# One program for attention, routing scores and experts, with one plan of memory and the first routed tiles turned in attention's tail

## The chip, the cores and the metric

The kernel runs on one core of a Trainium2 chip. The metric is the device time of one execution in microseconds; less is better. A core has five engines that run their own instruction queues and meet through semaphores: TensorE (PE; matmuls and transposes), VectorE (DVE), ScalarE (ACT), GpSimd (POOL) and SyncE (SP), which here issues nearly all transfers (DMAs) between DRAM and the core's memory, SBUF. Results of TensorE land in PSUM, eight banks of 128 partitions by 512 fp32 numbers.

## The reference

Input x is 4 batches of 1024 tokens of 512 numbers, fp32 throughout.

```python
# attention, 16 heads of 32, with biases; then residual and layernorm
x = _layernorm(x + _L0_attn_ref(x, wq, bq, wk, bk, wv, bv, wo, bo))
# routed and shared feed-forward
scores = xf @ gate_w.T                      # 8 experts
ew, ei = jax.lax.top_k(scores, 2); ew = softmax(ew)
expert_out = (silu(xf @ w_gate[e].T) * (xf @ w_up[e].T)) @ w_down[e].T   # H = 256
routed = weighted sum of the two chosen experts
shared = silu(xf @ sh_gate.T) * (xf @ sh_up.T) @ sh_down.T               # HS = 512
sgate = sigmoid(xf @ se_gate_w.T)
x = _layernorm(x + routed + sgate * shared)
```

## The kernel before

Tokens are handled in tiles of 128, TT = 32 tiles in all, eight (KT) to a batch. Where precision matters, an operand is split into a high part of a faster format and the low remainder, and three matmuls take the place of one.

The kernel is a row of programs, each a `nc.Block` of its own: inside a block the engines run freely by semaphores, and a block ends for all engines together before the next one begins. SBUF and PSUM of a stage are given back at its end and handed out anew to the next.

**Attention** (`attention`, L117 on). Per batch, four groups g of four heads (16 key steps of four slots each: `batch` on each engine), then a tail. SyncE's order is written out by hand in `body` and `tail`: projections' inputs, row sums out and their reciprocals back (`few`, `invert`, L384 to L396), the stacked keys and queries. In the last batch the output weights, kept in DRAM as high and low part (one megabyte each), are fetched at the end of group 1 into x_hi and x_lo (L433). In the tail, TensorE makes eight output tiles, 12 matmuls each (`o_tile`, L734 to L737). For every tile VectorE adds the residual and takes statistics (L1021 to L1029), GpSimd raises the variance to the power -0.5 and makes the shift (L561, L563), ScalarE normalises (L876), and SyncE stores it to x2 in DRAM (`store`, L460). The first four tiles of the last batch are kept in probs_mid. SyncE ends with a wait for all stores.

**Identity.** A small block of `moe` makes a second identity matrix on GpSimd (L2062, L2064).

**Routing scores** (`scores`). Tiles are taken four at a time, eight groups q. SyncE loads x2's tiles into four slots x_r (L1139). TensorE turns a tile by four transposes (`turn`, L1178, into pr_t). ScalarE copies the high part (`high`, L1227), VectorE subtracts for the low part (`low`, L1250). TensorE then makes the scores of four tiles with 12 matmuls (`score`, L1189), VectorE copies them (L1259), TensorE turns them back (`back`, L1200), and VectorE reads them into `route` (L1263). TensorE's order is written out in `group`: turn the next four tiles, scores of these, back of the last four. SyncE's order: router matrix (9 rows, L1142), tiles 0 to 3, one megabyte of shared weights (L1145), tiles 4 to 7, the other two megabytes (L1150), the rest of the tiles, each as its slot has been turned. GpSimd clears the router matrix (L1158) and splits the shared weights, 12 pieces of two operations (L1164, L1166). At the end ScalarE takes one tanh for the shared gate (L1241).

**Feed-forward** (`feed_forward`). SyncE loads tiles 0 to 3 into x_t (L1457), then eight experts' weights, twelve megabytes (L1474, L1475). Twelve tiles of the shared part (COVER = 12) run on TensorE: `turn` (L1572), `up` (24 matmuls, L1578), `down` (12), `turn_hidden` (L1603). Beside them VectorE chooses experts and builds the table of which token sits in which slot (`first_choice` and so on, from L1893), in many small operations. Then come 71 tiles of experts, in order of expert, and the other 20 shared tiles, with the results gathered and normalised.

## Time and profile before

| | us |
|---|---|
| median of 3 runs | 2098.14 (2097.38 to 2098.63) |
| the profiled execution's own time | 2099.2 |
| its span, first to last instruction | 2097.5 |
| TensorE busy | 2018.8 |
| VectorE busy | 1278.3 |
| ScalarE busy | 880.3 |
| GpSimd busy | 868.1 |

Mean granted clock of TensorE: 0.988 of full speed. Times in the trace count from the first instruction. The profile tells for each instruction its line, engine, start and duration, and for idle time in brackets how long the engine had been idle and what it waited for. In the rows, L12 is line 12 of the kernel; `out<-in` are the tensors written and read. A row with x4 merges four instructions in a row. A row of a stage gives its length, then the busy time of PE, PE's weight loads, DVE, ACT and POOL, and then three numbers: TensorE's granted clock (1.00 is 2.4 GHz, 0.50 is 1.2 GHz), the busy share of the 16 DMA engines, and what they moved in GB/s.

### The profile page before, as it was taken

To read this page: it belongs to the slowest core of one execution; us is meant where nothing else is said; L and a number is where in the kernel's file an instruction comes from. 1 tells how busy PE (TensorE), PEld (TensorE's weight loads), DVE (VectorE), ACT (ScalarE), POOL (GpSimd) and SP (SyncE) were. 2 spreads that over 40 slices of the span, in tenths; PEclk is the share of its full clock that TensorE was granted. 3 is DMA by queue.
4 is the path that set the end of the run, shared out by engine and by line. 5 is a ranking of instruction groups with operands and counts; after the bars stand their busy time and mean duration, and the time that the engine had idled before them with its cause. 6 is when DMAs were issued, how large, how long until landed. Compare 5 with 4: busy or idle time off the path is not lost. (4 is left out here: it accounts for less than half of the span.)

```text
span 2097.5 us, 30323 instructions
## 1 busy us (share of the span) xinstructions
PE 2018.8 (96%) x9764; PEld 1226.9 (58%) x9765; DVE 1278.3 (61%) x2281; ACT 880.3 (42%) x1563; POOL 868.1 (41%) x831
## 2 busy tenths in 40 slices
PE   7999999999999999999999986899999999999997
PEld 5655556655556655556655435588544444447886
DVE  5777775777776677775677855574222222225875
ACT  2266664466664466663466672321111111112332
POOL 3255654556654556653554555200111111114651
PEclk9999999999999999999999998999999999999999
DMA  7322434331434231335131305642222222225752
GB/s 231 71 53 55 100 78 107 115 69 42 101 76 131 92 76 47 97 67 163 60 77 33 91 12 201 221 186 66 90 90 88 86 87 89 90 80 166 229 175 74
DMA packets 95923, 213.00 MB, mean 102 GB/s; under 512 B 24305, under 2 KB 24817, under 8 KB 92593
## 3 DMA queue, kind: packets, MB, share of 16 engines
q1 hardware_dynamic: 84992, 175.96, 28.3%
q0 software_dynamic: 10800, 35.40, 6.2%
q8 instruction: 70, 1.15, 0.2%
q14 instruction: 61, 0.49, 0.1%
HBM read 118.51 MB, written 41.93 MB: 76 GB/s over the span
## 5 line engine op out<-in xcount | busy, mean ns | idle before, releaser
L947 DVE TENSOR_REDUCE max_half<-ps_side 128x1 f32<-128x512 f32 x1024 | 658.2, 682 | 204.6 <-PE ps_side L666 201.4
L666 PE MATMUL ps_side<-kq_stack 96*128 96x512 f32 x1024 | 409.4, 404 | 4.9 <-DVE max_half L947 2.4
L688 PE MATMUL ps_s<-kq_stack 97*128 97x512 f32 x937 | 393.0, 420 | 8.0 <-ACT probs_first L843 5.1
L688 PEld LDWEIGHTS ps_s<-kq_stack 97*128 97x128 f32 x937 | 177.8, 190 | 165.0 <-issue 85.5
L1636 PE MATMUL ps_gu<-gu_sb,xT_e 128*128 x568 | 257.7, 596 | 0.5 <-issue 0.3
L1534 POOL DMA_INDIRECT x_g<-x,who_all x71 | 67.3, 948 | 454.7 <-PE ps_t L1626 358.4
L843 ACT ACTIVATE probs_first<-ps_s 128x512 f32<-128x512 f32 x326 | 187.6, 600 | 106.0 <-PE ps_s L688 90.5
L666 PEld LDWEIGHTS ps_side<-kq_stack 96*128 96x128 f32 x1024 | 195.2, 191 | 57.8 <-DVE max_half L947 26.5
L843 ACT ACTIVATE probs_mid<-ps_s 128x512 f32<-128x512 f32 x308 | 177.5, 599 | 112.0 <-PE ps_s L688 97.4
L590 POOL TENSOR_TENSOR acc<-probs_first,probs_mid 128x512 f32<-128x512 f32 x129 | 163.8, 1297 | 133.2 <-ACT probs_mid L843 133.2
L843 ACT ACTIVATE probs_last<-ps_s 128x512 f32<-128x512 f32 x303 | 175.5, 599 | 97.2 <-PE ps_s L688 81.0
L590 POOL TENSOR_TENSOR acc<-probs_last,probs_first 128x512 f32<-128x512 f32 x129 | 163.3, 1292 | 116.6 <-ACT probs_first L843 116.6
L590 POOL TENSOR_TENSOR acc<-probs_mid,probs_last 128x512 f32<-128x512 f32 x118 | 149.6, 1295 | 109.8 <-ACT probs_last L843 109.4
L1757 ACT ACTIVATE act_g<-ps_gu 128x256 f32<-128x256 f32 x71 | 27.2, 383 | 346.6 <-PE ps_gu L1636 346.6
L1834 DVE TENSOR_TENSOR hid<-act_g,ps_gu 128x256 f32<-128x256 f32 x71 | 29.9, 421 | 221.7 <-ACT act_g L1757 221.7
L1636 PEld LDWEIGHTS ps_gu<-gu_sb,xT_e 128*128 128x128 f32 x568 | 102.3, 190 | 106.3 <-issue 106.0
L712 PE MATMUL ps_sum<-acc,ones 128*32 128x512 f32 x1024 | 134.7, 597 | 8.9 <-DVE acc L982 4.9
L1659 PE MATMUL ps_d<-wd_sb,act_g 128*128 x284 | 133.7, 593 | 0.5 <-DVE act_g L1841 0.5
L640 PE MATMUL ps_side<-x_hi,wkq_hi 128*128 128x512 f32 x256 | 103.0, 402 | 12.1 <-DVE x_lo L1036 10.5
L1847 DVE COPY y_t<-ps_d 128x512 f32<-128x512 f32 x71 | 49.1, 691 | 93.5 <-PE ps_d L1659 93.5
L1578 PE MATMUL ps_gu<-sgu_hi,xT_hi 128*128 128x512 f32 x256 | 104.0, 406 | 1.5 <-DVE xT_lo L1804 1.5
L640 PE MATMUL ps_side<-x_lo,wkq_hi 128*128 128x512 f32 x256 | 102.2, 399 | 0.0
(237 smaller groups left out, 3312.0 us busy)
## 6 DMA issues: line engine op xcount, KB each, us to landing
kq_stack<-kq SPq DMA_DIRECT2D x192, 256.0 KB, 5.1
y_slots<-y_t SPq DMA_DIRECT2D x71, 256.0 KB, 2.3
x_r<-x SPq DMA_DIRECT2D x32, 256.0 KB, 3.7
x_t<-x SPq DMA_DIRECT2D x32, 256.0 KB, 2.9
gu_sb<-wgu SPq DMA_DIRECT2D x8, 1024.0 KB, 16.1
out<-gu_sb SPq DMA_DIRECT2D x32, 256.0 KB, 2.7
res<-inv_rows SPq DMA_DIRECT2D x124, 64.0 KB, 2.0
stage<-wkqT SPq DMA_DIRECT2D x28, 256.0 KB, 3.0
```

Source lines behind the costliest of these rows:

```text
L590: nc.gpsimd.tensor_tensor(acc[:, h, :], probs(loc - 1, h), probs(loc, h), ALU.add).then_inc(folded, 1)
L640: done = nc.tensor.matmul(bank, w, xs, start=r == 0, stop=r == UNIT - 1)
L666: nc.tensor.matmul(bank, q_stack[par][0:3 * HD, h, t * P:(t + 1) * P], k_stack[par][0:3 * HD, h, half * HALF:(half + 1) * HALF], start=Tru ...
L688: nc.tensor.matmul(out, k_stack[par][0:3 * HD + 1, h, kt * P:(kt + 1) * P], q_stack[par][0:3 * HD + 1, h, half * HALF:(half + 1) * HALF], ...
L712: done = nc.tensor.matmul(ps_sum[h * HD:(h + 1) * HD, :], ones[:], acc[:, h, :], start=kt == FOLD - 1, stop=kt == KT - 1)
L843: nc.scalar.activation(probs(loc, h), score_bank(b, loc * HG + h)[0], ACT.Exp, scale=HD ** -0.5).then_inc(probs_ready, 1)
L947: nc.vector.reduce_max(max_half[:, u // 2, u % 2:u % 2 + 1], bank, AX.X).then_inc(side_free, 1)
L1534: nc.gpsimd.indirect_dma_start(x_g[:, t % 4, :], None, x2, bass.IndirectOffsetOnAxis(ap=who_all[:, t:t + 1].bitcast(U32), axis=0),).then_i ...
L1578: done = nc.tensor.matmul(out, w, m, start=c == 0 and i == 0, stop=c == last_c and i == 2)
L1636: done = nc.tensor.matmul(ps_gu[:, s % 2, :], e_xT[:, s % 2, c, :], gu_sb[:, bass.ds(e, 1), c, :].rearrange("p a n -> p (a n)"), start=c = ...
L1659: done = nc.tensor.matmul(ps_d[:, s % 2, :], e_hT[:, s % 2, c, :], wd_sb[:, bass.ds(e, 1), c, :].rearrange("p a n -> p (a n)"), start=c == ...
L1847: nc.vector.tensor_copy(y_t[:, s, :], ps_d[:, s % 2, :]).then_inc(ey_done, 1)
```

## The change

All stages stand in one block. Each engine's program is the three stages' programs one behind the other, with no meeting of engines between them. Memory is given out for routing and feed-forward first, and attention's buffers are laid over the same addresses in an order chosen so that what the next stages need early lies over what attention is done with early. One identity matrix serves all.

Of the work around the old joins, this is moved:

- In the last batch the output weights are fetched at the beginning of group 3 (`load_last`), into the keys' part of kq_stack0. Behind them, in the same place, come the router matrix and tiles 0 to 3 for the routing scores.
- In attention's last tail SyncE issues the first megabyte of shared weights ahead of the stores, the loads of tiles 4 to 7 behind the store of output tile 5, tiles 8 to 11 behind the last store, then the other two megabytes and the rest of the routed tiles.
- TensorE turns routed tiles 0 to 7 behind the eighth output tile. ScalarE copies their high parts: tiles 0 to 3 behind the normalisation of output tile 5, tiles 4 to 7 behind that of tile 7. VectorE makes the low parts behind its last output tile, and the router matrix's low part behind output tile 2.
- The eight groups of `scores` start with the scores of tiles 0 to 3 and turn tiles from group 1 on.
- The output tiles 0 to 3 of the last batch are kept in place in probs_first (`res_of`).
- Feed-forward's first four tiles are loaded as routed tiles 28 to 31 have been turned; its expert weights behind the last split of the shared weights.

```diff
-def attention(nc, x, xT, wkqT, wvT, woT, bq, bk, bv, bo, x2, passed):
+def attention(nc, keep, block, ident, router, x, xT, wkqT, wvT, woT, bq, bk, bv, bo, x2, passed):
...
-        def res_of(t):
-            return probs_mid[:, t, :] if t < 4 else x_of(t)
-        block = ctx.enter_context(nc.Block())
+        def res_of(b, t):
+            return probs_mid[:, t, :] if t < 4 and b < B - 1 else x_of(t)
...
+            def load_r(t):
+                sp.dma_start(router.x_t[:, t % 4, :], x2[t // KT, t % KT * P:(t % KT + 1) * P, :]).then_inc(
+                    router.x_in[t % 4], 16)
+
+            def load_shared(k):
+                sp.dma_start(router.stage[:, k], router.shared[k]).then_inc(router.st_in[k], 16)
+
+            def load_last(b):
+                sp.wait_ge(scores_ready, b * HEADS_B + (G - 1) * STEPS * HG)
+                sp.sem_inc(passed, 1)
+                for i, part in enumerate(wo_last):
+                    sp.dma_start(part.bitcast(F32), wo_kept[i]).then_inc(wo_in, 16)
+                sp.wait_ge(router.rw_zero, 1)
+                sp.dma_start(router.rw_raw[:, :, 0:E + 1], router.rw).then_inc(router.rw_in, 16)
+                for t in range(4):
+                    sp.wait_ge(x2_out[t], 16 * 2)
+                    load_r(t)
+
             def body(b, m, g, last):
+                if last and g == G - 1:
+                    load_last(b)
...
-                if last and g == 1:
-                    sp.wait_ge(proj_ready, PROJ * B * G)
-                    sp.sem_inc(passed_sp, 1)
-                    for i, part in enumerate((x_hi, x_lo)):
-                        sp.dma_start(part[:, :, 0:D].bitcast(F32), wo_kept[i]).then_inc(wo_in, 16)
...
                 load_x_nat(b, 3, res[:])
-                for t in range(KT):
+                if not last:
+                    for t in range(KT):
+                        store(b, t)
+                    return
+                sp.wait_ge(scores_ready, B * HEADS_B)
+                sp.sem_inc(passed, 1)
+                load_shared(0)
+                for t in range(6):
                     store(b, t)
+                for t in range(4, 8):
+                    sp.wait_ge(router.t_ready, t - 3)
+                    load_r(t)
+                for t in range(6, KT):
+                    store(b, t)
+                for t in range(8, 12):
+                    sp.wait_ge(router.t_ready, t - 3)
+                    load_r(t)
+                for k in range(1, 3):
+                    load_shared(k)
+                for t in range(12, TT):
+                    if t >= (B - 1) * KT:
+                        sp.wait_ge(x2_out[t % KT], 16 * (B + 1))
+                    sp.wait_ge(router.t_ready, t - 3)
+                    load_r(t)
...
-            for t in range(KT):
-                sp.wait_ge(x2_out[t], 16 * (B + 1))
...
+                    if last and g == G - 1 and at == 0:
+                        pool.wait_ge(proj_ready, PROJ * B * G)
+                        nc.gpsimd.memset(router.rw_raw[:], 0.0).then_inc(router.rw_zero, 1)
...
             for t in range(KT):
                 o_tile(b * TAIL + KT + t, b, t, tail_bank(t),
-                       [x_hi[:, g, 0:D] for g in range(G)], [x_lo[:, g, 0:D] for g in range(G)])
+                       [wo_last[0][:, g, :] for g in range(G)], [wo_last[1][:, g, :] for g in range(G)])
+            pe.wait_ge(probs_ready, B * HEADS_B)
+            pe.wait_ge(ctx_taken, INVERSES)
+            pe.wait_ge(sum_taken, INVERSES)
+            for q in range(2):
+                for s in range(4):
+                    router.turn(pe, q, s)
+            pe.wait_ge(tail_free, B * TAIL)
...
+            act.wait_ge(router.rw_in, 16)
+            nc.scalar.activation(router.rw_hi[:], router.rw_raw[:], ACT.Copy).then_inc(router.rw_high, 1)
             for t in range(KT):
                 norm(B - 1, t)
+                if t == 5:
+                    for s in range(4):
+                        router.high(act, 0, 0, s)
+            for s in range(4):
+                router.high(act, 1, 1, s)
...
                 if t < 2:
                     ctx_low_last(t)
+                if t == 2:
+                    dve.wait_ge(router.rw_high, 1)
+                    nc.vector.tensor_tensor(router.rw_lo[:], router.rw_raw[:], router.rw_hi[:].bitcast(F32),
+                                            ALU.subtract).then_inc(router.rw_split, 1)
+            for q in range(2):
+                for s in range(4):
+                    router.low(dve, q, q, s)
...
+class Router:
+    def turn(self, pe, q, s):
+        t = 4 * q + s
+        pe.wait_ge(self.x_in[s], 16 * (q + 1))
+        if not static(q, 1):
+            pe.wait_ge(self.t_hi, t - 3)
+            pe.wait_ge(self.t_lo, t - 3)
+        for c in range(C):
+            done = self.nc.tensor.transpose(self.ps_t[:, s, c * P:(c + 1) * P], self.x_t[:, s, c * P:(c + 1) * P],
+                                            self.ident[:])
+        done.then_inc(self.t_ready, 1)
...
-        block = ctx.enter_context(nc.Block())
...
             for t in range(4):
+                sp.wait_ge(router.t_ready, TT - 3 + t)
                 load_tile(t)
+            sp.wait_ge(router.st_split, 3 * C)
+            sp.sem_inc(passed, 1)
             for e in range(E):
...
+        with nc.Block() as block:
+            attention(nc, keep, block, ident, router, x, xT, wkqT, wvT, woT, bq, bk, bv, bo,
+                      x2.rearrange("(b s) d -> b s d", b=B), passed)
+            scores(nc, block, router, weights_hi_lo, route, sgate_all, ident, passed)
+            feed_forward(nc, keep, block, router, memory, x2, sgu_hi, sgu_lo, sd_hi, sd_lo, wgu, wd, base, y, gu_sb,
+                         wd_sb, route, sgate_all, weights, pos, tile_expert, ident, out, passed)
```

## Rows read from the trace of the kernel before

**Rows 1.** The page, part 1: busy us, share of the span, instructions.

```profile
PE 2018.8 (96%) x9764; PEld 1226.9 (58%) x9765; DVE 1278.3 (61%) x2281; ACT 880.3 (42%) x1563; POOL 868.1 (41%) x831
```

**Rows 2.** Busy time by stage, from:to, length, PE, PEld, DVE, ACT, POOL, clock, DMA, GB/s.

```profile
1283.60:1294.80 11.20, 0.01 (x1) 0.01 (x1) 2.01 (x6) 1.88 (x3) 1.52 (x6) 0.70 0.33 94
1294.80:1314.82 20.02, 15.89 (x76) 10.26 (x77) 8.93 (x14) 7.17 (x12) 13.51 (x16) 0.82 0.90 339
1314.82:1344.87 30.05, 29.37 (x182) 17.42 (x180) 17.64 (x34) 10.51 (x20) 8.59 (x9) 1.00 0.47 146
1344.87:1351.16 6.29, 1.12 (x5) 0.75 (x5) 1.22 (x4) 1.71 (x3) 2.38 (x6) 0.61 0.67 197
1351.16:1359.17 8.01, 8.01 (x24) 6.33 (x25) 2.80 (x8) 0.43 (x1) 0.00 (x0) 0.67 1.01 411
```

**Rows 3.** The chain that ended last: start us, us, work; a later feed-forward tile.

```profile
1404.66 5.54 PE ps_gu L1578 x24
```

**Rows 4.** TensorE in order of time at the first join: start us, us, work.

```profile
1282.50 1.07 PE L737 MATMUL ps_side<-x_lo,kq 128*128 128x512 f32 x4
...
1294.79 1.12 PE L1178 MATMUL pr_t<-ident_m,x_r 128*128 128x128 f32 x4 [11.22 <-DMA x_r<-x]
...
1296.07 2.66 PE L1178 MATMUL pr_t<-ident_m,x_r 128*128 128x128 f32 x12 [0.16 <-DMA x_r<-x]
...
1309.18 2.58 PE L1178 MATMUL pr_t<-ident_m,x_r 128*128 128x128 f32 x16 [1.33 <-DMA x_r<-x]
...
1311.52 0.48 PE L1189 MATMUL pr_s<-xT_hi_r,rw_hi 128*16 128x512 f32 x1
...
1314.82 2.28 PE L1178 MATMUL pr_t<-ident_m,x_r 128*128 128x128 f32 x16
```

**Rows 5.** VectorE and ScalarE in order of time, first join and a steady group.

```profile
1283.60 0.69 DVE L1021 TENSOR_TENSOR res<-ps_side,res 128x512 f32<-128x512 f32 x1 [0.76 <-PE ps_side L737]
...
1285.41 0.14 DVE L1029 TENSOR_SCALAR var_eps<-mv 128x1 f32<-128x1 f32 x1
...
1286.49 0.81 ACT L876 ACTIVATE res<-res,shift,rstd 128x512 f32<-128x512 f32 x1 [1.90 <-POOL shift L563]
...
1315.51 2.22 ACT L1227 ACTIVATE xT_hi_r<-pr_t 128x512 fp32r<-128x512 f32 x4 [3.12 <-PE pr_t L1178]
...
1316.14 2.48 DVE L1250 TENSOR_TENSOR xT_lo_r<-pr_t,xT_hi_r 128x512 fp32r<-128x512 f32 x4 [0.78 <-ACT xT_hi_r L1227]
```

**Rows 6.** The routed tiles' loads (x_r), from issue to landing.

```profile
DMA to landing us min/median/max: 2.6/3.7/6.9
```

**Rows 7.** Busy time in single microseconds, columns as in rows 2.

```profile
1288.00:1289.00 1.00, 0.00 (x0) 0.00 (x0) 0.00 (x0) 0.00 (x0) 0.00 (x0) 0.59 0.70 262
...
1298.00:1299.00 1.00, 0.72 (x5) 0.48 (x3) 0.84 (x2) 0.84 (x2) 0.00 (x0) 0.79 1.00 422
```

**Rows 8.** Busy time in a stretch full of transfers, columns as in rows 2.

```profile
1295.00:1308.00 13.00, 10.07 (x44) 6.94 (x43) 5.64 (x9) 4.78 (x8) 7.01 (x8) 0.74 1.02 399
```

**Rows 9.** GpSimd in order of time: the last splitting operation of the shared weights.

```profile
1322.43 1.30 POOL L1166 TENSOR_TENSOR sd_lo<-wd_sb,sd_hi 128x512 fp32r<-128x512 f32 x1
```

**Rows 10.** ScalarE and TensorE in order of time at the second join.

```profile
1345.13 0.26 ACT L1241 ACTIVATE th<-route 128x32 f32<-128x32 f32 x1 [6.95 <-DVE route L1263]
...
1348.54 1.12 PE L1572 MATMUL ps_t<-ident_m,x_t 128*128 128x128 f32 x4 [3.68 <-DMA x_t<-x]
...
1349.69 0.60 ACT L1730 ACTIVATE xT_hi<-ps_t 128x512 fp32r<-128x512 f32 x1 [4.30 <-PE ps_t L1572]
```

**Rows 11.** SyncE's queue and VectorE in the last group of attention.

```profile
1213.07 3.07 SPq L384 DMA_DIRECT2D sum_few<-res  x4
...
1227.02 0.24 DVE L970 RECIPROCAL inv_few<-sum_few 128x16 f32<-128x16 f32 x1
```

**Rows 12.** Groups by line (page, part 5): ScalarE's exponentials by target buffer.

```profile
L843 ACT ACTIVATE probs_first<-ps_s 128x512 f32<-128x512 f32 x326 | 187.6, 600 | 106.0 <-PE ps_s L688 90.5
...
L843 ACT ACTIVATE probs_mid<-ps_s 128x512 f32<-128x512 f32 x308 | 177.5, 599 | 112.0 <-PE ps_s L688 97.4
```

More of the change, by code:

```diff
@@ new lines, in attention @@
+        kq_stack = [sb(f"kq_stack{i}", [P, 2, HG, S], F32R) for i in range(2)]
+        x_hi = sb("x_hi", [P, C, S], F32R)
+        x_lo = sb("x_lo", [P, C, S], F32R)
+        wkq_hi = sb("wkq_hi", [P, 2, C, P], F32R)
+        wkq_lo = sb("wkq_lo", [P, 2, C, P], F32R)
+        wv_hi = sb("wv_hi", [P, C, D], F32R)
+        acc, wo_hi = twin("acc", "wo_hi", [P, HG, HALF])
+        v_sb = sb("v_sb", [P, KT, D])
+        probs_last, wo_lo = twin("probs_last", "wo_lo", [P, HG, HALF])
+        probs_mid, wv_lo = twin("probs_mid", "wv_lo", [P, HG, HALF])
@@ new lines, in sem @@
+            return keep.enter_context(nc.semaphore(name))
+        self.nc, self.ident, self.stage, self.shared, self.rw = nc, ident, stage, shared, rw
+        self.x_t = sb("x_r", [P, 4, D])
+        self.rw_raw = sb("rw_raw", [P, C, RW])
+        self.rw_hi = sb("rw_hi", [P, C, RW], F32R)
+        self.rw_lo = sb("rw_lo", [P, C, RW], F32R)
+        self.xT_hi = sb("xT_hi_r", [P, 2, C, 4 * P], F32R)
+        self.xT_lo = sb("xT_lo_r", [P, 2, C, 4 * P], F32R)
+        self.sT = sb("sT", [RW, 2, 4 * P])
@@ new lines, in __init__ @@
+        self.th = sb("th", [P, TT])
+        self.ps_t = space.enter_context(nc.psum_tensor("pr_t", [P, 4, D], F32))
+        self.ps_s = space.enter_context(nc.psum_tensor("pr_s", [P, 2, 4 * P], F32))
+        self.ps_b = space.enter_context(nc.psum_tensor("pr_b", [P, 4, RW], F32))
+        self.st_in = [sem(f"st_in{i}") for i in range(3)]
+        self.st_high = sem("st_high")
+        self.st_split = sem("st_split")
+        self.rw_zero, self.rw_in, self.rw_high, self.rw_split = [
+            sem(f"rw_{n}") for n in ("zero", "in", "high", "split")]
@@ L1169, in _ @@
         def _(pe):
-            def turn(q, s):
-                t = 4 * q + s
-                pe.wait_ge(x_in[s], 16 * (q + 1))
-                if not static(q, 1):
-                    pe.wait_ge(t_hi, t - 3)
-                    pe.wait_ge(t_lo, t - 3)
-                for c in range(C):
-                    done = nc.tensor.transpose(ps_t[:, s, c * P:(c + 1) * P], x_t[:, s, c * P:(c + 1) * P], ident[:])
-                done.then_inc(t_ready, 1)
             def score(q, g):
@@ L1203, in group @@
             def group(q, g, first, last):
+                if not first and not last:
+                    for s in range(4):
+                        r.turn(pe, q + 1, s)
                 if first:
-                    for s in range(4):
-                        turn(q, s)
-                if not last:
-                    for s in range(4):
-                        turn(q + 1, s)
-                if first:
-                    pe.wait_ge(rw_split, 1)
+                    pe.wait_ge(r.rw_split, 1)
                 score(q, g)
@@ L1265, in group @@
             def group(q, g, first, last):
-                if first:
-                    low(q, g)
-                if not last:
-                    low(q + 1, 1 - g)
+                if not first and not last:
+                    for s in range(4):
+                        r.low(dve, q + 1, 1 - g, s)
                 take(q, g)
@@ L1584, in up @@
                 pe.wait_ge(t_lo, t + 1)
+                if t == 0:
+                    pe.wait_ge(router.st_split, 2 * C)
                 if t >= 1:
```

320 lines of the change are left out of this document (136 added, 184 removed).

## The prediction

> **What bounds the kernel now.** First the page: TensorE is busy for 96% of the span [rows 1]. That is an average over stages, so the next view is the table of busy time by stage, cut at the two joins which the change touches [rows 2]. Its first row runs from the end of the last output matmul to the first transpose of the routing scores. It is 11.2 us long and TensorE has nothing in it. In the second row (20.0 us up to the fourth group of scores) TensorE works 15.9 us, at a mean clock of 0.82. The third row is steady: busy 29.4 of 30.05 us, full clock. The fourth and fifth are the second join, 6.3 us with 1.1 us of work and then 8.0 us of matmuls at a mean clock of 0.67, where a later tile takes 5.5 us for the same 24 [rows 3]. Away from the joins TensorE is the bound, and the change leaves its matmuls as they are. So the question is how much of these 45.5 us (11.2 + 20.0 + 6.3 + 8.0) remains.
>
> **First join, before.** The output matmuls end at 1283.57. Transposes of routed tile 0 begin at 1294.79, of tiles 8 to 11 at 1309.18; the second scores begin at 1311.52, and turning tiles 12 to 15 at 1314.82 [rows 4]. Ahead of it stand VectorE's statistics of the last output tile, ScalarE's normalisation at 1286.49, its store, the barrier, the identity, and only then the loads [rows 4, 5].
>
> **First join, after, on the clock of the old trace.**
> 1. *Tiles 0 to 3.* Their rows in DRAM are two batches old, and SyncE fetches them in the last group of attention. TensorE turns them right behind the last output matmul. Twelve transposes at half clock took 2.66 us, so sixteen at full clock take 1.8, and sixteen in a steady group, with waits in them, 2.28 [rows 4]. These wait for nothing, so I take 1.8: 1283.6 to 1285.4.
> 2. *Tiles 4 to 7* need their slot loaded again. SyncE issues a load when the transpose of its slot is done, 1284.2 for the first. x_r loads landed in 2.6 to 6.9 us, 3.7 at the median [rows 6]. The long ones stood behind a megabyte of weights, and that megabyte (shared weights, part 0) now moves behind the last input load of the tail, well before. I take 2.9 us, near the low end: 1287.1, then one each 0.5 us. The transposes also need the slot's low half off VectorE, which is free at 1285.55 [rows 5] and does four in 2.48 [rows 5]: 1286.2 to 1288.1. So 1287.1 to 1289.2. The bounds are 2.6 and 6.9 us: 0.3 us better, 4 us worse.
> 3. *ScalarE* puts four copies (2.22 us, [rows 5]) ahead of the normalisation of output tile 6. It waits for the first transposes at 1284.2, is done at 1286.4, and normalises tiles 6 and 7 by 1288.0, where tile 7 ended at 1287.3. Behind these two stand only their stores and the loads of tiles 8 to 11, issued from 1288.6 to 1290.1 and landed by 1293.2. TensorE wants them about then.
> 4. *First scores*, 12 matmuls. The second ones with the four small transposes back took 3.30 [rows 4], of which the transposes are some 0.35, so 2.95 alone. The clock: after 4.6 us without work it was at half from about 1288.2 [rows 7]. The new gap has transposes in it, 1.8 us and then 2 us of thinly spread ones in 5.6 us. I expect the clock to fall once and to be back within these scores: 3.8 us, 1289.2 to 1293.0. With a clock that holds it would be 2.95, with a low one to the end twice that, 5.9; I stay nearer to the first, since the work no longer stops.
> 5. *Tiles 8 to 11, scores 1, back:* 2.34 + 3.30 as before [rows 4], to 1298.6.
> 6. *Tiles 12 to 15* are issued behind the other two megabytes of shared weights (issued at 1290.6). At 399 GB/s [rows 8] these take 5.3 us, to about 1296.5, and tiles 12 to 15 are there from 1297.6 to 1299.6. That just fits, at a bound of 2 us if it does not. Turning of tiles 12 to 15 starts at 1298.6, not at 1314.82: **16.2 us gained**.
>
> From there the group is TensorE's own, as in the third row of [rows 2].
>
> GpSimd's 24 splitting operations of the shared weights ended at 1323.7 [rows 9]. They now begin at about 1286.5 instead of 1300.7 and pause for the second megabyte, so they end near 1313 and nobody waits. VectorE's one small subtraction (0.23 us) behind output tile 2 and ScalarE's 0.26 us copy lie in slack: VectorE idled 0.76 us ahead of the last tile [rows 5]. Cost nothing.
>
> **Second join.** Before: the scores end at 1344.87, the loads of the feed-forward tiles are issued only behind the barrier, tile 0 is turned at 1348.54, ScalarE copies at 1349.69, VectorE subtracts, and the first matmul starts at 1351.16, 1.47 us behind the copy's start [rows 2, 10]. Now the four loads are issued while tiles 28 to 31 are turned, more than one group of 5 us (the third of [rows 2] holds six) ahead of the end, and the last lands in time unless it takes the whole 6.9. TensorE turns tile 0 at once: four transposes, 0.5 us, to 1345.4. ScalarE has its tanh at 1345.13 for 0.26 [rows 10] and is free. It copies from 1345.4, and 1.47 us on the first matmul starts, at 1346.9: **4.3 us gained**. The 24 matmuls took 8.0 us at a mean clock of 0.67, and take 5.54 at full clock [rows 2, 3]: **2.4 us more** if the clock holds. TensorE stands for 1.5 us there, behind four transposes; before, it stood for 3.68 [rows 10], and the clock fell. I count some chance that it falls again for part of the matmuls, and take 1.9. VectorE's first choice of experts (with the subtraction 2.80 us and more in the last row of [rows 2]) still fits under 5.5 us of matmuls. The twelve megabytes of expert weights start some 10 us earlier by the same clock, behind the four tile loads and the splitting. They are needed twelve shared tiles later, so this earns nothing and delays nothing.
>
> **What moves inside attention.** SyncE's queue of the last batch gets seven transfers (two megabytes of output weights, one of routed tiles, the small router matrix) ahead of the row-sum transfers which it issued at 1213.07. Issue costs some 4 us. The three megabytes at 399 GB/s need 7.9 us [rows 8, 11]. So the sums arrive at about 1222, and VectorE takes their reciprocal at 1227.02, without having waited [rows 11]. About 5 us of cover remain; each microsecond over it would hold VectorE and with it TensorE. GpSimd's clearing of the router matrix is 0.15 us. Cost nothing.
>
> **Sum:** 16.2 + 4.3 + 1.9 = 22.4 us off the profiled execution, whose span is 2097.5 and whose time is 2099.2. The median of the runs is 1.06 lower than that execution, 2098.14; less 22.4 gives **2075.7 us**. By the bounds of steps 2, 4 and 6 and of the second join the gain lies between 16 and 25.
>
> The Trainium skill, TensorE: Matmul & The Clock Gate, "Part 4: PE-mode transpose", says that the engine's transposes do not count as activity for the clock. The trace speaks against it here: between 1294.8 and 1298.9 TensorE ran transposes alone, and the clock went from half to full at about 1298.4 [rows 4, 7]. By the page the first scores would run wholly at half clock (5.9 us for 3.8), and the gain would be 2.1 us smaller; by the row I leave it.
>
> **Rivals.**
> - *The loads replace the barrier* (chance 0.13). Tiles 4 to 7 land at the median or later, or tiles 12 to 15 wait for the weights, and both joins run at half clock. For: in the second row of [rows 2] the transfer engines are 0.90 busy. Against: the first megabyte has left that stretch. Price 5 us or so: gain 17.4, 2080.7.
> - *The row sums come late* (0.04). Three megabytes stand ahead of them; if they took twice the estimate, the sums would come at about 1230, plus the time to reach the next reader: 3 to 10 us lost, 2079 to 2086. Against: nothing else of size moves there.
> - *Placement* (0.03), the slower side. All attention buffers have other addresses. If the long stage, 1283.6 us, ran slower by 1.75% or more, the whole gain would be gone; at 2.2% the time would be 2103.9. Against: ScalarE's exponentials into different buffers take 600 and 599 ns [rows 12].
> - *The joins do not open* (0.02): some wait still orders the engines as the barrier did, by SyncE's order of stores and loads. Then the time stays within 4 us of 2098.
>
> **Numbers.** The forecast has 0.78, its own range 2072.5 to 2079. The range of 8 in 10 takes in most of the first rival: 2071.5 to 2081. A difference of 0.2%, some 4.2 us, is about what a measurement of this kernel can tell from none. Faster by more than that hold the forecast, the first rival and most of the second, 0.95; within it 0.02; slower 0.03.
>
> **What would show it.** Right: the time from the last output matmul to the turning of tile 12 falls from 31.25 to about 15 us, no wait of pr_t on x_r over 3 us; the scores' end to the end of the first 24 matmuls falls from 14.3 to about 8; attention ends where it did, at 1283.6, with the reciprocal at about 1227 not waiting. Wrong: DVE idle ahead of inv_few in the last group, a second long wait on x_r, a clock at half into the second group of scores, or exponentials off 600 ns.

## The result, and the profile after

The changed kernel takes **2083.45 us** by the median of four runs (2079.12 to 2085.13), beside 2098.39 for the kernel before on the same chip: a ratio of 0.9925 with a 95% interval of 0.9909 to 0.994, or 15 us less. Forecast were 2075.7, range 2071.5 to 2081.0. The profiled execution is the fastest of the four, 2079.12 us with a span of 2077.4, so it must not be set against the forecast by itself.

The page's part 1 of the changed kernel, which answers to [rows 1]:

```profile
PE 2010.8 (97%) x9764; PEld 1220.1 (59%) x9765; DVE 1278.2 (62%) x2281; ACT 880.1 (42%) x1563; POOL 868.2 (42%) x829
```

The same 9764 matmuls run. TensorE in order of time at the first join, as in [rows 4]; the value in brackets is the idle time ahead and what ended it:

```profile
1277.07 1.07 PE L771 MATMUL ps_side<-kq_stack,kq 128*128 128x512 f32 x4
1277.98 1.91 PE L1197 MATMUL pr_t<-ident,x_r 128*128 128x128 f32 x16
1281.16 1.35 PE L1197 MATMUL pr_t<-ident,x_r 128*128 128x128 f32 x8 [1.27 <-DMA x_r<-x]
1283.88 1.97 PE L1197 MATMUL pr_t<-ident,x_r 128*128 128x128 f32 x8 [1.37 <-DMA x_r<-x]
1285.50 0.78 PE L1249 MATMUL pr_s<-xT_hi_r,rw_hi 128*16 128x512 f32 x1
...
1289.14 1.91 PE L1197 MATMUL pr_t<-ident,x_r 128*128 128x128 f32 x16
...
1295.71 2.95 PE L1197 MATMUL pr_t<-ident,x_r 128*128 128x128 f32 x16 [1.53 <-DMA x_r<-x]
...
1302.79 1.97 PE L1197 MATMUL pr_t<-ident,x_r 128*128 128x128 f32 x16
```

The 11.2 us without work are gone: the first sixteen transposes stand right behind the last output matmul. In their place are three shorter waits, all put down to the rows of routed tiles (4 and 5, 6 and 7, 12 to 15). SyncE's queue in the same stretch, and the busy time by windows (columns as in [rows 2]):

```profile
1278.61 1.74 SPq L394 DMA_DIRECT2D x_r<-x  x4
1281.40 1.02 SPq L493 DMA_DIRECT2D x<-res  x2
1282.47 3.73 SPq L394 DMA_DIRECT2D x_r<-x  x4
1286.24 1.11 SPq L398 DMA_DIRECT2D wd_sb<-shu  x1
1287.40 0.43 SPq L398 DMA_DIRECT2D wd_sb<-shd  x1
1289.77 1.86 SPq L394 DMA_DIRECT2D x_r<-x  x4
```

```profile
1278.00:1285.00 7.00, 4.32 (x30) 3.62 (x29) 5.46 (x11) 4.53 (x8) 4.78 (x9) 0.91 0.80 265
...
1284.00:1287.00 3.00, 3.00 (x12) 2.10 (x13) 1.18 (x2) 1.19 (x2) 2.92 (x4) 0.50 0.91 279
...
1298.00:1301.00 3.00, 3.00 (x11) 1.32 (x10) 1.76 (x3) 1.04 (x2) 2.84 (x5) 0.52 0.91 264
```

Tiles 4 to 7 are asked for between 1278.6 and 1280.4, and TensorE gets the third of them only at 1283.9. The first row below is from the issue to the landing of the last two of these loads. The second is the same for tiles 26 and 27, and the third for tiles 18 and 19 in the kernel before, both in stretches where four such loads move by themselves (187 and 184 GB/s):

```profile
DMA to landing us min/median/max: 4.4/4.4/4.5
DMA to landing us min/median/max: 4.0/4.0/4.1
DMA to landing us min/median/max: 3.9/3.9/4.0
```

So the third and fourth of four loads issued in a row take about 4 us here with nothing beside them; the stores and loads behind tiles 4 to 7 add some 0.4. Tiles 12 to 15 stand in the queue behind two megabytes of weights. And the clock goes to half twice (0.50 and 0.52, the level of 1.2 GHz), each time after one of these waits: the first scores and the third group of scores pay for it. The second join, with the busy time by windows up to the first feed-forward matmul and over the first 24:

```profile
1327.21:1329.26 2.05, 0.59 (x6) 0.38 (x5) 1.17 (x4) 1.67 (x3) 0.00 (x0) 1.00 1.01 424
1329.26:1334.80 5.54, 5.54 (x25) 4.54 (x26) 2.85 (x8) 0.47 (x1) 0.00 (x0) 1.00 1.01 417
```

Here 6.29 and 8.01 us [rows 2] became 2.05 and 5.54. VectorE's reciprocal of the row sums, which the second rival was about, waited for nothing. Below are SyncE's issue of the four transfers of sums, their time to landing, and the reciprocal:

```profile
1215.28 3.15 SPq L378 DMA_DIRECT2D sum_few<-res  x4
DMA to landing us min/median/max: 5.8/6.4/6.6
1224.47 0.24 DVE L1018 RECIPROCAL inv_few<-sum_few 128x16 f32<-128x16 f32 x1
```

The last of them is issued at 1217.2 and lands 6.6 us later, at 1223.8: 0.7 us ahead of the reciprocal, where some 5 us of cover were forecast.

So that stages can be added up, the next table is cut at the same matmuls in the traces of all kernels run, one profiled execution each. "Attention" is from the first matmul to the end of the last output matmul; "join 1" from there to the end of all routing scores; "wait" to the first feed-forward matmul; "first 24" these matmuls; "experts" from there over the loop of the experts' tiles to a down projection of the first shared tile behind it, "exit" the 14 matmuls from that one to the start of the third such tile. "Median" is of the timed runs, "ratio" against the kernel before on the same chip; medians from different chips are compared by it. What is behind the exit, to the start of the last matmul, took 167.72 to 167.81 us in all.

| kernel | attention | join 1 | wait | first 24 | experts | exit | median | ratio |
|---|---|---|---|---|---|---|---|---|
| before | 1273.02 | 61.29 | 6.30 | 8.02 | 557.17 | 2.66 | 2098.39 | 1 |
| after | 1267.46 | 49.07 | 2.05 | 5.53 | 559.27 | 4.82 | 2083.45 | 0.9925 |
| again | 1273.69 | 48.50 | 2.05 | 7.19 | 559.09 | 3.97 | 2084.75 | 0.992 |
| pad1 | 1272.10 | 49.60 | 2.05 | 5.55 | 559.21 | 2.66 | 2082.43 | 0.9914 |
| pad2 | 1272.21 | 50.94 | 2.05 | 5.57 | 559.30 | 3.99 | 2083.28 | 0.9917 |
| pad7 | 1271.14 | 50.88 | 2.05 | 7.15 | 559.12 | 2.66 | 2084.19 | 0.9921 |
| padl3 | 1272.26 | 48.03 | 2.05 | 7.15 | 559.30 | 3.95 | 2083.53 | one run |
| padl40 | 1269.58 | 48.49 | 2.05 | 7.19 | 564.15 | 3.97 | 2086.38 | one run |
| drain | 1275.00 | 49.08 | 2.22 | 7.00 | 559.30 | 2.66 | 2083.93 | 0.9928 |
| split | 1266.80 | 50.41 | 6.23 | 7.38 | 556.87 | 3.99 | 2085.94 | 0.9933 |
| late | 1267.08 | 54.26 | 2.05 | 7.16 | 559.14 | 2.66 | 2084.23 | 0.9929 |
| v1 | 1271.56 | 48.34 | 2.05 | 7.01 | 559.48 | 3.98 | 2080.60 | 0.9905 |
| v2 | 1276.00 | 44.69 | 2.05 | 7.16 | 559.10 | 2.66 | 2078.19 | 0.9894 |
| v12 | 1270.45 | 43.08 | 2.05 | 8.44 | 559.30 | 2.66 | 2076.76 | 0.9892 |
| v12p3 | 1271.17 | 43.38 | 2.05 | 5.55 | 559.40 | 2.66 | 2075.15 | 0.9887 |
| v12d | 1267.00 | 43.81 | 2.22 | 7.15 | 559.35 | 2.66 | 2078.01 | 0.9909 |
| v24p3 | 1274.01 | 45.27 | 2.04 | 7.08 | 559.31 | 2.66 | 2079.93 | 0.9901 |

The first two rows account for the profiled executions: 5.6 in attention, 12.2, 4.25 and 2.5 at the joins, less 2.1 in the stage of the experts and 2.2 at the exit, is 20.3 of the 20.1 us between the spans. The runs' medians differ by 15. The experiments ask which of these terms are the change's.

### The profile page after: what moved, and what is told of

It reads as the page before. It is cut to its first block, busy times and chain, and to the rows that moved or that the text cites. A ratio compares the mean times of both kernels' runs of the same rounds, so it can differ in the third digit from the quotient of the medians.

```text
span 2077.4 us, 30213 instructions
## 1 busy us (share of the span) xinstructions
PE 2010.8 (97%) x9764; PEld 1220.1 (59%) x9765; DVE 1278.2 (62%) x2281; ACT 880.1 (42%) x1563; POOL 868.2 (42%) x829
## 4 chain that ended last, share of the span: by engine, by line
PE 84%; SPq 4%; DMA 3%; DVE 3%; issue 2%; POOL 2%; ACT 1%; ACTq 0%; DVEq 0%; POOLq 0%
PE ps_gu L1679 12%; PE ps_s L722 11%; PE ps_side L700 11%; PE ps_ctx L733 10%; PE ps_side L674 8%; PE ps_gu L1617 8%; PE ps_d L1702 6%; PE ps_sum L746 5%; PE ps_d L1617 4%; SPq L359 3%; DMA inv_rows<-inv_few 2%; PE ps_t L1669 1%; PE pr_s L1249 1%; DVE max_half L995 1%; PE ps_side L722 1%
## 5 line engine op out<-in xcount | busy, mean ns | idle before, releaser
L674 PE MATMUL ps_side<-x_hi,wkq_lo 128*128 128x512 f32 x256 | 101.8, 398 | 0.0
```

What stands on the lines that cost most here:

```text
L674: done = nc.tensor.matmul(bank, w, xs, start=r == 0, stop=r == UNIT - 1)
```

## The experiments

### The kernel again: how much of the 20 us is the execution's

> The changed kernel, run again. Its profiled execution had the end of the last output matmul at 1278.14 where the kernel before had 1283.57, because two falls of the granted clock inside attention (1015.1 for 3.4 us and 1240.4 for 6.8 us) were absent. Theory (chance of the execution, not of the change): a second profiled execution shows falls inside attention at other places, or none, and the end of the last output matmul anywhere from 1278 to 1285; the time of the median execution stays at 2082 to 2085. Rival (the new placement of the buffers keeps the clock up): the end of the last output matmul is again within 0.7 us of 1278.1, with no fall between 100 and 1275 us, and the median is nearer to 2080. In both, the first join (last output matmul to the end of its four groups' scores) is 49.1 within 1 us, and the loss in the experts' loop (about 2 us in the loop and 2 at its exit against the kernel before) is there again.

Measured: 2084.75 us by the median of six (2080.37 to 2087.35), ratio 0.992 (0.9906 to 0.9935). Attention took 1273.7 us, as in the kernel before, with two stretches at half clock inside it (from 394 and from 1018 us) where the first trace had none. Over the sixteen profiled executions with the change (late and the v kernels below move loads at its end) it lies between 1266.8 and 1276.0, 1271.1 in the mean; the kernel before, at 1273.0 in its one trace, is inside. So the 5.6 us are mostly luck, and an effect of the change on attention, if there is one, is too small to see in this spread. Join 1 is 48.5, as expected.

### The second join's barrier put back (split)

```
+        with nc.Block() as block:
             feed_forward(nc, keep, block, router, memory, x2, ...
```

> The feed-forward and experts get their own block again, so the barrier of the second join is back and the first join stays as changed. Theory (the second join's gain is the barrier's): the pause of TensorE between the scores' end and the first feed-forward matmul goes from 2.05 back to 6.3 us and the clock falls during the 24 matmuls of the first tile (8.0 for 5.5 us): 6.7 us slower, about 2090. Rival (the gain came from loads that are early, and the barrier costs little): 2 us slower or less. The place of the experts' loop moves too, so up to 4 us less of the loss may be left, and the stretch itself decides, not the time.

TensorE in order of time:

```profile
1331.58 1.12 PE L1611 MATMUL ps_t<-ident,x_t 128*128 128x128 f32 x4 [3.66 <-DMA x_t<-x]
...
1334.15 0.77 PE L1617 MATMUL ps_gu<-sgu_hi,xT_hi 128*128 128x512 f32 x1 [1.46 <-ACT xT_hi L1773]
```

The wait of [rows 10] (3.68) is back as 3.66, the pause is 6.23, the first 24 matmuls take 7.38. The 4.2 us of the pause are the barrier's, as the theory says. The whole kernel, expected at 2090, is only 1.2 us slower by the median than again's (intervals 0.992 to 0.9946 and 0.9906 to 0.9935, which overlap), and two reasons are in the table: with the barrier the stage of the experts is 2.2 to 2.6 us shorter, and the first 24 matmuls are only 0.2 us shorter in again, whose clock fell there too (7.19 us for 7.38).

### The first four tiles loaded late (late)

```
-                for t in range(4):
-                    sp.wait_ge(x2_out[t], 16 * 2)
-                    load_r(t)
...
-                for t in range(4, 8):
-                    sp.wait_ge(router.t_ready, t - 3)
+                for t in range(8):
+                    if t >= 4:
+                        sp.wait_ge(router.t_ready, t - 3)
                     load_r(t)
```

> The first four routed tiles are loaded behind the store of output tile 5 rather than in the last group of attention; the barrier stays away. Theory (the transposes behind the last output matmul wait for nothing only because their rows were fetched early): the loads are issued at about the end of the last output matmul less 1 us and land 2.6 to 3.7 us later, so the turning starts 2 to 3 us after the last output matmul, not at it, and tiles 4 to 7 come as much later: 2.5 us slower, about 2086. Rival (what follows, tiles 4 to 7 and the weights, is late by the transfers anyway): under 1 us slower.

```profile
1279.78 4.24 PE L1195 MATMUL pr_t<-ident,x_r 128*128 128x128 f32 x20 [2.09 <-DMA x_r<-x]
1285.54 1.30 PE L1195 MATMUL pr_t<-ident,x_r 128*128 128x128 f32 x8 [1.52 <-DMA x_r<-x]
1287.16 1.11 PE L1195 MATMUL pr_t<-ident,x_r 128*128 128x128 f32 x4 [0.32 <-DMA x_r<-x]
...
1300.05 3.45 PE L1195 MATMUL pr_t<-ident,x_r 128*128 128x128 f32 x16 [2.14 <-DMA x_r<-x]
```

The start comes 2.09 us late, but join 1 grew by 5.2 (54.26, against 49.08, the median of the eight kernels that leave it as changed): the wait adds to the others, and the clock was at half four times up to the first feed-forward matmuls. The early load is worth 5 us in this trace, twice what was expected. The median, 2084.23 where 2086 was expected, is not clearly apart from the changed kernel's; the stretch is, since the eight that leave it as changed reach 50.94 at most.

### What TensorE waits for in the first join (v1, v2, v12, v24p3)

v1 moves two transfers:

```
-                for k in range(1, 3):
-                    load_shared(k)
                 for t in range(12, TT):
+                    if t in (16, 20):
+                        load_shared(t // 4 - 3)
```

> The second and third megabyte of shared weights are loaded behind the routed tiles 15 and 19, not ahead of tile 12. Theory (tiles 12 to 15 wait behind these two megabytes, 1.53 us, and TensorE's wait lets the clock fall, which makes the scores after it slower by 1.75): the wait of the turning of tiles 12 to 15 on their rows vanishes and the scores after it run at full clock: 1.5 to 3.3 us faster, about 2081. Rival (the tiles wait for their own 256 KB transfers, not for the weights): the wait stays over 1 us and the time within 0.5 us of 2083.5. If GpSimd's splitting of the shared weights ends too late, the first feed-forward tile waits instead; it has some 15 us of slack.

```profile
1297.77 1.96 PE L1197 MATMUL pr_t<-ident,x_r 128*128 128x128 f32 x16
1304.51 3.44 PE L1197 MATMUL pr_t<-ident,x_r 128*128 128x128 f32 x16 [1.65 <-DMA x_r<-x]
```

Tiles 12 to 15 no longer wait, so the weights were what they waited for. The median is 2080.60, beside 2084.75 for again on the same chip, with intervals of the ratios that overlap (0.9891 to 0.9919 and 0.9906 to 0.9935). But tiles 16 to 19 do wait, behind the megabyte that now stands ahead of them, with the clock at half. Join 1 is 48.34, only 0.7 under the median of 49.08: the wait moved. What the median of the runs gained is not shown by this trace. v2 gives tiles 4 to 7 their own buffer:

```
+                x_t = router.x_t2 if 4 <= t < 8 else router.x_t
...
+                for t in range(4, 8):
+                    sp.wait_ge(router.x_in[t - 4], 16)
+                    load_r(t)
                 load_shared(0)
                 for t in range(6):
                     store(b, t)
-                for t in range(4, 8):
-                    sp.wait_ge(router.t_ready, t - 3)
+                for t in range(8, 12):
+                    sp.wait_ge(router.x_in[t - 8], 32)
+                    sp.wait_ge(router.t_ready, t - 7)
                     load_r(t)
...
-                for t in range(8, 12):
-                    sp.wait_ge(router.t_ready, t - 3)
-                    load_r(t)
+                sp.wait_ge(router.t_ready, 8)
...
```

> Tiles 4 to 7 of the routed rows get a buffer of their own, are loaded in the tail of attention ahead of the stores, and tiles 8 to 11 are loaded as soon as tiles 0 to 3 are turned; the shared weights still stand ahead of tile 12. Theory (the two waits of 1.2 to 1.5 us on tiles 4 to 7, and the thin work in them, cost 1.8 us more than predicted): both waits go, the first scores begin 4 us behind the last output matmul rather than 6.1 to 7.4, and 2 to 3 us are gained if the wait of tiles 12 to 15 doesn't grow by as much. Rival (the transfers are the bound: three megabytes ahead of tile 12): the wait of tiles 12 to 15 grows by what the earlier ones lose, and the sum from the last output matmul to the end of the scores stays at 47 to 49.6.

```profile
1286.51 1.91 PE L1203 MATMUL pr_t<-ident,x_r 128*128 128x128 f32 x16
1289.41 2.42 PE L1203 MATMUL pr_t<-ident,x_r 128*128 128x128 f32 x16 [0.99 <-DMA x_r<-x]
1294.48 1.91 PE L1203 MATMUL pr_t<-ident,x_r 128*128 128x128 f32 x16
1301.07 2.41 PE L1203 MATMUL pr_t<-ident,x_r 128*128 128x128 f32 x16 [1.56 <-DMA x_r<-x]
```

The scores begin 5.0 us behind the last output matmul instead of 7.4 (6.1 to 7.4 in the eight kernels); the wait for tiles 12 to 15 is 1.56 (1.5 to 3.7 in those) and did not grow, so the transfers are not the bound. Join 1 is 44.69, 4.4 less than their middle. The clock did not fall here, but it did not in again either, and join 1 is 3.8 less than again's 48.50, nearly all of it up to the turning of tile 12 (14.4 us behind the last output matmul for 18.1). A wait of 0.99 is left at tile 4. It can't be the load's, which was issued at 1270.1 and landed within 5.8 us; in v12 the same wait is put down to VectorE's lower halves. So of the changed kernel's first wait, 1.27 us, the load was worth some 0.3, and VectorE bounds the rest.

> Both: tiles 4 to 7 in a buffer of their own, and the second and third megabyte of shared weights behind the routed tiles 15 and 19. By the theory all waits of the turning on its rows go but one behind a megabyte of weights (1.65 us in v1 at tiles 16 to 19, shorter here since nothing else is late): 44.5 us from the last output matmul to the end of the scores, where the changed kernel has 47.1 to 49.6, and a time of 2079.5. If the transfers are the bound, 47 us and 2081 to 2082, as v1.

```profile
1280.90 1.91 PE L1203 MATMUL pr_t<-ident,x_r 128*128 128x128 f32 x16
1283.80 2.42 PE L1203 MATMUL pr_t<-ident,x_r 128*128 128x128 f32 x16 [0.99 <-DVE xT_lo_r L1218]
1288.88 1.91 PE L1203 MATMUL pr_t<-ident,x_r 128*128 128x128 f32 x16
1293.85 1.97 PE L1203 MATMUL pr_t<-ident,x_r 128*128 128x128 f32 x16
```

With both edits join 1 takes 43.08 us (43.38 and 43.81 in its two variants below), 5.3 to 6.0 less than the changed kernel and at least 4.2 less than the shortest of the eight, and the medians are 2076.76, 2075.15 and 2078.01. That settles the cause of most of join 1's loss: the rows of the routed tiles, late behind their own slot and behind the weights. The expectation had join 1 shorter by 2.6 to 5.1 and the time at 2079.5, and was too cautious in both. (The expectations of v2 and v12 and that of v12p3 count join 1 to the start of the last group's transposes back, 1.4 us less than the table: by that count v12 has 41.7 and v12p3 42.0.)

v24p3 is v12p3 (below) with the third megabyte behind tile 23 instead of tile 19:

> As v12p3, with the third megabyte of shared weights behind routed tile 23 rather than 19. In v12 no turning waited for its rows, so there is nothing to gain at the routing scores: the time within 1 us of v12p3. If GpSimd's splitting of that megabyte then ends behind the first feed-forward tile's need (1320 in the changed kernel), the first feed-forward matmuls wait and it is slower by up to 5 us.

2079.93 us and 45.27 for join 1: nothing gained over v12p3, as said, but the time is 4.8 us over v12p3's median where 1 was expected. The waits of 0.4 and 0.8 us that reappear at tiles 16 to 23 were not explained, and the difference between the medians is inside the spread of runs (2074.24 to 2084.38).

### The experts' loop

Four experts' tiles make one turn of TensorE's loop. In order of time, the changed kernel, then split (the first ps_hts of each is the last before the jump back):

```profile
1504.87 0.38 PE L1692 MATMUL ps_hts<-ident,hid 128*128 128x128 f32 x2
1505.26 3.70 PE L1679 MATMUL ps_gu<-gu_sb,xT_e 128*128 x8
1510.95 0.38 PE L1692 MATMUL ps_hts<-ident,hid 128*128 128x128 f32 x2
1511.22 3.70 PE L1679 MATMUL ps_gu<-gu_sb,xT_e 128*128 x8
1516.91 0.38 PE L1692 MATMUL ps_hts<-ident,hid 128*128 128x128 f32 x2
```

```profile
1511.19 0.38 PE L1692 MATMUL ps_hts<-ident,hid 128*128 128x128 f32 x2
1511.57 3.70 PE L1679 MATMUL ps_gu<-gu_sb,xT_e 128*128 x8
1517.25 0.38 PE L1692 MATMUL ps_hts<-ident,hid 128*128 128x128 f32 x2
1517.47 3.63 PE L1679 MATMUL ps_gu<-gu_sb,xT_e 128*128 x8
1523.09 0.38 PE L1692 MATMUL ps_hts<-ident,hid 128*128 128x128 f32 x2
```

The tile behind the jump takes 6.08 and 6.06 us, the next 5.96 and 5.84: the loss sits in that second tile alone. Over fifteen turns the mean is 23.648 us in the changed kernel, 23.516 in split, 23.531 in the kernel before. Split keeps the changed placement of all buffers, so that is not the cause. Six kernels tried the obvious one, the place of the code. pad1, pad2 and pad7 stand so many increments at the start of TensorE's program, v12p3 three on v12, padl3 and padl40 in the feed-forward's own part:

```
+            for i in range(2):
+                pe.sem_inc(passed, 1)
```

> Two instructions that do nothing (increments of a counter) stand at the start of TensorE's program, in idle time, so that every later instruction of TensorE lies two places further, where the kernel before had it (its loop over the experts starts at place 4963, the changed kernel's at 4961). Theory (the loss in the experts' stage comes from where the loop's code lies): the extra 0.115 us of each iteration at its second slot's first projection and the 1.5 us stall without a named releaser at the loop's exit change or vanish; the experts' stage is 3 to 4 us shorter, the time 2079 to 2081 by the median. Rival (the loss comes from what the loop meets: memory placement, the earlier loads): nothing changes, 2083.5, the stall at the exit is 1.5 us and the loop keeps its 2 us.

> One instruction that does nothing at the start of TensorE's program, where pad2 had two. In pad2 nothing changed, and in split, whose one more block moves the loop's code by another amount, the extra 0.117 us per iteration of the experts' loop was gone (23.516 us for four iterations' matmuls, 23.64 with it), the stall at the exit was not. Theory (the jump back costs more or less by where its target lies, and two places further is as bad as none): with one place the loop needs 23.52 again, 2.0 us less in all, and the exit's gap stays or goes. Rival (in split the barrier took the loss away by its timing, not by the place of the code): the loop stays at 23.64. The time would be 2081.5 in the one case, 2083.5 in the other, which the intervals can hardly tell; the sum of the loop's iteration in the trace decides.

> Seven do-nothing instructions at the start of TensorE's program. In the built programs the experts' loop starts at instruction 6479 of TensorE in the kernel before and 6476 in split, which have the short iteration (23.52 for four), and at 6473, 6474 and 6475 in the changed kernel, pad1 and pad2, which have the long one (23.64). Theory A (the jump back costs by the place of its target in eights): with seven the loop starts at 6480, the first of an eight as 6473 to 6475 are in its first half, and the iteration is long, 23.64. Theory B (in fours, or by something that only changes between 6475 and 6476): short, 23.52. Rival C (the barrier's timing): long as well, so the run with three decides between A and C.

> v12 with three do-nothing instructions at the start of TensorE's program: the loop starts at 6476, where split had it, with no barrier. Theory (the place of the code): four iterations take 23.52, 2.0 us less in all than in v12, and the time is 2075. Rival (the barrier's timing took the loss away in split): 23.64 and 2077. The joins as in v12: 41.7 us from the last output matmul to the end of the last pr_s group's matmuls within 1 us.

> The changed kernel with three do-nothing instructions of TensorE ahead of the experts' loop, in the feed-forward's own part of its program (v12p3 had three at the start of the program and kept the long iteration, 23.646; split has three more instructions at the join and the short one, 23.516). If the place of the code within its part decides, four iterations take 23.52; if not, 23.64, and small shifts of TensorE's code are excluded at both places, so that split's short iteration is the barrier's doing or that of a larger difference in the built program.

> As padl3 with forty. They move the loop against the blocks of 16 KB in which the trace shows TensorE's instructions arriving. If such a block's border inside the loop makes the iteration long, 40 places change it (23.52, or another value than 23.64); if neither the fine nor the coarse place matters, 23.64 again and the time as the changed kernel's plus under 1 us.

Turns of the loop: 23.641, 23.639, 23.637, 23.646, 23.644, 23.643. None is short; the theory of the code's place fell at every size tried. (v12p3's median, 2075.15, is what that theory had forecast, by luck: its turn stayed long.) What the barrier does to TensorE itself was the next guess (drain, v12d: `pe.drain()`, which lets TensorE's queue run empty ahead of the first feed-forward tile):

> The changed kernel with a drain of TensorE alone ahead of the first feed-forward tile: TensorE's queue runs empty there, as it does at the barrier of the kernel before and of split, and no other engine is held. In the trace of the changed kernel the sequencer of TensorE takes up the look-up of the second slot's expert 0.113 us later than in split, and the matmul that needs it waits. Theory (where the queue stands in relation to the loop is set by the last time it ran empty): the iteration is 23.52 per four, 2.0 us less in all, and the time 2082 or less. Rival (the barrier matters by holding the other engines, or it is something else in the built program): 23.64, and the time 2083.5 to 2084.5.

> v12 with the same drain. By the theory 23.52 per four iterations and 2075; by the rival 23.64 and 2077. The joins as in v12.

23.647 and 23.640: that fell too. In the traces of both states the instructions of the loop are the same; the sequencer of TensorE (the part that reads its program) takes up the look-up of the second tile's expert some 0.12 us later without the barrier (4.91 for 4.79 us behind the first matmul of the tile ahead, in the mean of fifteen turns), and the tile takes as much longer. Why is **open**. The two kernels with the barrier have the short turn, the fifteen without it the long one; whether it matters by holding the other engines wasn't tried.

The exit is another matter. The changed kernel has a stall there, ahead of the third shared tile behind the loop, that the trace puts down to nothing:

```profile
1898.88 0.47 PE L1617 MATMUL ps_gu<-sgu_hi,xT_hi 128*128 128x512 f32 x1 [1.51 <-issue]
```

Again, pad2, split and v1, which ran on one chip, have 1.3 us of it, and so have padl3 and padl40; pad1, v2, v12 and late, on another, have none, nor have pad7, v12p3, v24p3, drain and v12d. Among the kernels with the change it goes with where and when they ran, whatever the kernel. The kernel before has no stall in its one trace, so whether it would have one where again ran is open, and so is the changed kernel's own, 2.2 us.

padl40 cost 4.9 us more in "experts" where under 1 was expected, and the trace shows the place, where padl3 with its three has no wait:

```profile
1462.04 1.08 PE L1669 MATMUL ps_t<-ident,x_g 128*128 128x128 f32 x4 [4.46 <-issue]
```

## Why the prediction was wrong

The sum was 22.4 us. Of the terms:

- **Attention, nothing:** right, but by less than it says. The reciprocal did not wait, and attention's length is inside the spread. The cover of 5 us was not there: the sums lay 0.7 us ahead of the reciprocal, and 0.6 to 1.8 in the other kernels that fetch tiles 0 to 3 in the same place. The sum had the three megabytes at 399 GB/s; from the first issue (1210.6) to the landing of tile 3 (1223.1) they took 12.5 us and not 7.9. The second rival was nearer than its 0.04.
- **Join 1, 16.2:** measured 12.2 (10.3 to 13.3 over the eight kernels that leave it as changed). Here is most of the miss. Step 1 was right to a tenth (1277.98, no wait). *Step 2* failed: "2.9 us, then one each 0.5 us" let the scores begin 5.6 us behind the last output matmul, and they began at 7.4 (6.1 to 7.4 over the eight). The first pair took 2.5 and 2.8 us to land, but the second pair 4.4 and 4.5 (3.6 to 4.6 over the eight), so tile 7 was there 6.3 us behind the last output matmul and not 5.0. That was in the old trace: its tiles 18 and 19 took 3.9 and 4.0 behind 16 and 17, with no other transfers near. The other 0.5 us are the half clock, under which tiles 6 and 7 were turned. Steps 4 and 5 were 0.2 and 0.6 us too pessimistic. *Step 6*, "just fits", did not: 1.5 to 3.7 us of wait in the eight kernels, 2.1 in the middle, where I had named a bound of 2. It counted the two megabytes' 5.3 us from their issue, while tiles 8 to 11 were still landing ahead of them, by step 3 until 1293.2: these two together would have given 1298.5 for the weights and a wait already. In the trace tile 11 lands at 1289.2 and the weights 5.6 us behind it, at 1294.8. And the sum stopped at the turning of tile 12, "from there the group is TensorE's own": behind that wait the clock fell once more, and the 30.05 us of [rows 2] became 31.5. Together 1.8 − 0.2 − 0.6 + 1.5 + 1.5 = 4.0.
- **Join 2, 4.3 + 1.9:** the pause was 4.25 shorter in each kernel without a barrier or drain, by the step's own working. For the matmuls 2.5 in the profiled execution, but in most others the clock fell once: the middle of the eight is 7.1 us, 0.9 less than before. So 5.2 rather than 6.2. v12p3, whose clock held, shows the best case.
- **Experts, unchanged:** wrong by 2.1 us, through something that no step had and that stays unexplained. The exit's 2.2 us in the profiled execution (0 to 1.3 in the others) were in no step either.

4.0 + 1.0 + 2.1 is 7.1 of the 7.75 us between 2075.7 and 2083.45. The range was too narrow as well: the bounds of steps 2, 4 and 6 and of the second join, all on the bad side, take 4 + 2.1 + 2 + 1.9 off 22.4 and leave 12.4 us, not 16. The joins together gave 17.4 us in the middle of these kernels, and that is what the first rival said (tiles 4 to 7 late or tiles 12 to 15 behind the weights, gain 17.4). I gave it 0.13. Its two causes came true, both of them, the half clock only in part (0.52 and 0.50 in two stretches of the first join, 1.00 in the second); that its round price of 5 us fits to a tenth is luck, and its time, 2080.7, was missed by 2.75, since the experts' loss was in no rival. The profile had spoken for it: in the second row of [rows 2] the transfer engines are 0.90 busy, and the new plan put more loads into less time. The other rivals did not show: attention stayed in its spread, the joins opened.

On the clock, in v12 TensorE ran transposes alone for the first 5 us of the join and stayed at full clock, as the window of that stretch shows (the clock is the third number from the end); through the matmuls behind them it kept it until 1326:

```profile
1280.90:1286.00 5.10, 4.11 (x33) 3.35 (x31) 4.65 (x10) 4.46 (x9) 2.96 (x7) 1.00 0.69 213
```

The Trainium skill, TensorE: Matmul & The Clock Gate, "Part 4: PE-mode transpose", says that transposes do not count as TensorE's activity in the way other work does, and that the full clock does not engage for them. The trace does not agree, as far as it goes: this stretch shows a clock that stays up, and only the old trace shows one that rises behind transposes alone. In the changed kernel each fall comes within 2 us of the end of a wait, but a wait did not always bring one: of the eight kernels, again and padl3 kept the clock all through join 1 with waits of 2.07 and 2.13 us at tile 12. What decides it is not shown.

## What to carry to other kernels

When a barrier goes, the work behind it is no longer late by the barrier but by its own transfers: write the queue's order with bytes and issue times for the whole stretch that moves forward, ask of each transfer what stands ahead of it, and take the landing of the third and fourth load from a row of such loads, not from the first. A second small buffer and two megabytes issued four and eight tiles later gave back another 6 us here (v12: 2076.76, ratio 0.9892 for 0.9925; v12p3, 2075.15, is the same but for three empty instructions). And compare profiled executions stage by stage before believing a total: attention varies by 8 us between executions of kernels that do the same there (1266.8 to 1275.0 without late and the v kernels).

## What had not been expected

Seven do-nothing increments of a counter at the start of TensorE's program, in idle time, cost nothing that shows (pad7), and three in the busy stream nothing either (padl3), but forty there stopped TensorE for 4.46 us. The experts' loop runs 0.5% longer in the fifteen kernels that passed no barrier some 140 us earlier than in the two that did, always at the same matmuls. And a short wait can cost twice: in the changed kernel the fall of the clock after it cost about as much as the wait (1.5 and 1.5 us at tiles 12 to 15), in again, with a wait of 2.07, nothing.
